# A fused metaformer block on one core: the order of three stages within a step, and the buffers and loads of the filling

## What is computed

```python
x1 = conv3x3(x[:, :12], w_pc)                      # on LayerNorm over channels
x  = conv1x1(concat([x1, x[:, 12:]]), w_in)        # 48 -> 254 channels
xf = rfft2(8x8 patches of x) * fft_w               # weights per channel and frequency
a, b = split(irfft2(xf))                           # 127 and 127 channels
x  = x_in + conv1x1(gelu(a) * b, w_out)            # 127 -> 48, residual
t  = tokens of x; q = fp8e5(LayerNorm(t))
h  = relu(f16(f16(q @ fp8e5(W1)) + b1))            # 48 -> 192
t  = t + f16(f16(fp8e5(h) @ fp8e5(W2)) + b2)       # 192 -> 48, residual
```

## Time and profile before

| | us |
|---|---|
| median of 3 runs | 762.5 |
| lowest and highest | 761.84 and 766.21 |
| the profiled execution, its own time | 763.09 |
| its span, first to last instruction | 761.3 |
| mean granted TensorE clock | 0.983 |

### The profile page before, as it was taken

One profiled execution on the slowest core, in us unless ns is written; L12 is line 12 of the kernel. 1 busy time (PEld: TensorE's weight loads), 2 busy tenths in 40 slices (PEclk: granted clock), 3 DMA queues, 4 the chain that ended last, 5 costly groups with the idle time before them and its releaser, 6 DMA issues.

```text
span 761.3 us, 20170 instructions
## 1 busy us (share of the span) xinstructions
PE 683.0 (90%) x6571; PEld 506.1 (66%) x6571; DVE 594.9 (78%) x1128; ACT 549.0 (72%) x1090; POOL 484.5 (64%) x356
## 2 busy tenths in 40 slices
PE   1349999999999999989999999999999999999952
PEld 1137776777777777667777777777777777776720
DVE  4616788888888888978888888888888888887751
ACT  3134477877878877867888777878788887766764
POOL 2544657777767777767767777776876776743342
PEclk9999999999999999999999999999999999999985
DMA  3343314443334333344344333334434342231001
GB/s 71 68 98 70 79 35 98 99 101 101 74 93 99 98 82 80 87 105 101 67 100 97 97 76 80 94 100 102 101 66 100 96 99 77 63 97 44 22 22 42
DMA packets 46501, 62.36 MB, mean 82 GB/s; under 512 B 19039, under 2 KB 34871, under 8 KB 46391
## 3 DMA queue, kind: packets, MB, share of 16 engines
q1 hardware_dynamic: 46151, 60.94, 33.1%
q10 hardware_dynamic: 240, 0.05, 0.1%
HBM read 44.62 MB, written 16.35 MB: 80 GB/s over the span
## 4 chain that ended last, share of the span: by engine, by line
PE 64%; issue 12%; ACT 8%; DVE 7%; DMA 3%; POOL 2%; SPq 2%; ACTq 1%; POOLq 0%; DVEq 0%
PE mixp L461 15%; PE inva L474 11%; PE invb L479 11%; PE misc L488 7%; PE misc L534 5%; ACT hid L687 4%; PE misc L507 3%; DVE zl L852 3%; PE misc L633 3%; PE misc L516 2%; ACT zh L731 2%; PE misc L611 2%; PE misc L560 2%; PE misc L575 1%; DVE gmix L863 1%
## 5 line engine op out<-in xcount | busy, mean ns | idle before, releaser
L863 DVE TENSOR_TENSOR gmix<-mixp,freq_w 128x508 f32<-128x508 f32 x256 | 163.6, 681 | 38.0 <-PE mixp L461 37.5
L474 PE MATMUL inva<-inv,gmix 128*127 128x128 f32 x1024 | 135.6, 275 | 1.6 <-DVE gmix L863 1.6
L678 ACT ACTIVATE hid<-misc 128x512 f16<-128x512 f32 x192 | 102.0, 621 | 47.3 <-PE misc L534 47.3
L479 PE MATMUL invb<-inv,gmix 128*127 128x128 f32 x1024 | 134.5, 274 | 0.0
L461 PE MATMUL mixp<-win,zh 60*128 60x254 f16 x1024 | 120.7, 273 | 15.3 <-DVE zl L852 13.1
L474 PEld LDWEIGHTS inva<-inv,gmix 128*127 128x127 f32 x1024 | 129.6, 192 | 5.2 <-issue 3.6
L479 PEld LDWEIGHTS invb<-inv,gmix 128*127 128x127 f32 x1024 | 123.8, 191 | 0.0
L1036 POOL TENSOR_TENSOR st<-st,neg_half 128x16 f32<-128x16 f32 x32 | 94.5, 2954 | 45.3 <-DVE st L953 45.3
L461 PE MATMUL mixp<-win,zl 60*128 60x254 f16 x1024 | 119.4, 268 | 0.0
L1067 POOL TENSOR_TENSOR st<-st,neg_half 128x16 f32<-128x16 f32 x32 | 92.8, 2900 | 37.5 <-DVE st L989 37.5
L687 ACT ACTIVATE hid<-hid 128x512 fp8e5<-128x512 f16 x192 | 106.8, 636 | 0.0
(11 more groups left out here) (104 smaller groups left out, 1146.9 us busy)
## 6 DMA issues: line engine op xcount, KB each, us to landing
xin<-in_x_dram SPq DMA_DIRECT2D x64, 192.0 KB, 3.4
xres<-in_x_dram SPq DMA_DIRECT2D x64, 192.0 KB, 4.2
out_dram<-ob SPq DMA_DIRECT2D x64, 192.0 KB, 3.5
taps<-cz_scratch SPq DMA_DIRECT2D x32, 292.5 KB
crm<-rm_scratch SPq DMA_DIRECT2D x64, 96.0 KB
cz_scratch<-cz SPq DMA_DIRECT2D x64, 48.8 KB
cx<-in_x_dram SPq DMA_DIRECT2D x32, 96.0 KB
rm_scratch<-rm_t SPq DMA_DIRECT2D x128, 4.0 KB
```

The source lines that it names most:

```text
L474: mm = pe.matmul(inva[0:HID, q * PX:(q + 1) * PX], gmix[:, s % 2, q, 0:HID], inv[:], start=True, stop=True, skip_group_check=True)
L479: mm = pe.matmul(invb[0:HID, q * PX:(q + 1) * PX], gmix[:, s % 2, q, HID:HID2], inv[:], start=True, stop=True, skip_group_check=True)
L678: act.activation(hid16[:, 3 * c + g, :], bank[banks[g]][:], ACT.Copy).then_inc(hid16_ready, 1)
L863: dve.tensor_tensor(gmix[:, s % 2, 2 * q:2 * q + 2, 0:HID2], mixp[q][:, 0:2 * HID2].rearrange("p (e c) -> p e c", e=2), freq_w[:], ALU.mul ...
```

## The change

Within a turn:

- ScalarE: the high halves `zh` are copied ahead of the conversions to `hid8`; the three conversions become one instruction of 128x1536 elements, here and at the other place.
- VectorE: both low halves `zl` (with the mean between them) come ahead of the tokens `qpix`; `weigh(t, 0)` comes ahead of `gate(t, 4, 3)` and of the bias on `y16`.
- TensorE: `mix(t, 0)` comes ahead of FFN2.

In the filling, and in the buffers: `xpix`, `cx` and `crm` get two buffers, and the waits are loosened by one turn (VectorE's three waits ahead of its first sum by six more); the loads of weights are regrouped over SyncE's and ScalarE's queues and over the turns; the padding's zeros go out in turn 1; the biases are loaded behind the row statistics of turn 1.

```diff
-        xpix = sb("xpix", [128, PAIRS, 128])
+        xpix = sb("xpix", [128, 2, PAIRS, 128])
...
-        cx = sb("cx", [CC * CG, 2 * W])
-        crm = sb("crm", [CC * CG, 2, 2 * W])
+        cx = sb("cx", [CC * CG, 2, 2 * W])
+        crm = sb("crm", [CC * CG, 2, 2, 2 * W])
...
@@ -305,7 +305,7 @@
 
             def load_cx(t, behind):
                 n = at(t, behind)
-                sp.dma_start(cx[:], x_rows[image(n), n % SPI, 0:CC]).then_inc(cx_in, 16)
+                sp.dma_start(cx[:, ring(t, behind)], x_rows[image(n), n % SPI, 0:CC]).then_inc(cx_in[ring(t, behind)], 16)
 
...
             load_x((0, 0), -1)
-            sp.dma_start(raw_fft[:], fft_w.rearrange("(g p) a b u v -> p g (a b u v)", g=2)).then_inc(const_in, 16)
+            load_cx((0, 0), -1)
+            with nc.allow_non_contiguous_dma(reason="small weights, once"):
+                for part in range(2):
...
             sp.dma_start(raw_in[:, :, 0:CC], w_in_rows[:, :, 0:CC]).then_inc(const_in, 16)
             sp.dma_start(raw_in[:, :, CC:KC], w_in_rows).then_inc(const_in, 16)
-            sp.dma_start(raw_out[:], w_out.rearrange("o c a b -> o (c a b)")).then_inc(const_in, 16)
             sp.dma_start(raw_w1[:], w1.rearrange("(g p) c -> p g c", g=2)).then_inc(const_in, 16)
             sp.dma_start(raw_w2[:], w2).then_inc(const_in, 16)
-            for dst, src in ((sel, sel_d), (fwd, fwd_d), (inv, inv_d)):
-                sp.dma_start(dst[:], src).then_inc(const_in, 16)
-
-
-            def setup():
+
+            def transforms():
+
+                for dst, src in ((sel, sel_d), (fwd, fwd_d), (inv, inv_d)):
+                    sp.dma_start(dst[:], src).then_inc(const_in, 16)
+
+            def biases():
 
                 sp.wait_ge(zeroed, 1)
-                with nc.allow_non_contiguous_dma(reason="small weights, once"):
-                    for part in range(2):
-                        for dx in range(3):
-                            sp.dma_start(raw_pc[part * 3 * CC:(part + 1) * 3 * CC, dx, :],
-                                         w_pc[:, :, :, dx].rearrange("o i dy -> (i dy) o")).then_inc(const_in, 16)
-
-            def biases():
-
                 with nc.allow_non_contiguous_dma(reason="small weights, once"):
                     sp.dma_start(raw_b[:, 0:1], b1[0:128].rearrange("(p o) -> p o", o=1)).then_inc(bias_in, 16)
...
-                sp.wait_ge(csub, upto(a))
+                sp.wait_ge(csub, upto(a - 1))
                 sp.sem_inc(sp_held, 1)
                 for kind in range(2):
                     src = rm_d[ring(t, 0), kind].rearrange("(g q) w -> g (q w)", g=CG)
-                    sp.dma_start(crm[:, kind, :], src.unsqueeze(0).to_broadcast([CC, CG, 2 * W]))\
-                      .then_inc(rm_in, 16)
+                    sp.dma_start(crm[:, ring(t, 0), kind, :], src.unsqueeze(0).to_broadcast([CC, CG, 2 * W]))\
+                      .then_inc(rm_in[ring(t, 0)], 16)
 
...
                 a, n, m, k, l = (at(t, d) for d in (0, 3, 4, 5, 6))
                 early = isinstance(t[0], int) and t[1] < 2
+                if early:
+                    rows_out(t)
+                    if a == 0:
+                        transforms()
                 if live(t, -1) and not (isinstance(t[0], int) and t[1] == 0):
                     sp.wait_ge(xord_ready, upto(a))
                     sp.sem_inc(sp_held, 1)
@@ -384,17 +386,13 @@
                     sp.sem_inc(sp_held, 1)
                     load_res(t, 3)
                 if early:
-                    if a == 0:
-                        setup()
-                    rows_out(t)
-                    if a == 0:
+                    rows_in(t)
+                    if a == 1:
                         biases()
-                if live(t, 0) and not (isinstance(a, int) and a == 0):
+                if live(t, -1) and not (isinstance(t[0], int) and t[1] == 0):
                     sp.wait_ge(cmul, upto(a))
                     sp.sem_inc(sp_held, 1)
-                    load_cx(t, 0)
-                if early:
-                    rows_in(t)
+                    load_cx(t, -1)
...
                 if live(t, 4):
                     inverse(t, 4, 3)
+                if live(t, 3):
+                    mix(t, 0)
                 if live(t, 6):
...
                         mm.then_inc(y_done, 1)
-                if live(t, 3):
-                    mix(t, 0)
                 if live(t, 4):
...
-            def activations(k, c, groups):
-
-                for g in groups:
-                    act.wait_ge(relu_ready, upto(6 * k + 3 * c + g + 1))
-                    if c == 0 and g == 0:
-                        act.wait_ge(y_done, upto(2 * k))
-                    act.sem_inc(act_held, 1)
-                    act.activation(hid8[:, 3 * c + g, :], hid16[:, 3 * c + g, :], ACT.Copy, saturate=False)\
-                       .then_inc(hid8_ready, 1)
+            def activations(k, c):
+
+                act.wait_ge(relu_ready, upto(6 * k + 3 * c + 3))
+                if c == 0:
+                    act.wait_ge(y_done, upto(2 * k))
+                act.sem_inc(act_held, 1)
+                act.activation(hid8[:, 3 * c:3 * c + 3, :], hid16[:, 3 * c:3 * c + 3, :], ACT.Copy, saturate=False)\
+                   .then_inc(hid8_ready, 3)
...
+            def pads():
+
+                act.wait_ge(row_zeroed, 1)
+                for part in range(2):
...
-            act.wait_ge(row_zeroed, 1)
...
+            act.dma_start(raw_out[:], w_out.rearrange("o c a b -> o (c a b)")).then_inc(const_in, 16)
+            act.dma_start(raw_fft[:], fft_w.rearrange("(g p) a b u v -> p g (a b u v)", g=2)).then_inc(const_in, 16)
             order_x((0, 0), 0)
...
                         if q == 0:
-                            act.wait_ge(xcen_ready, upto(a))
-                            act.wait_ge(sum1, upto(a))
+                            act.wait_ge(xcen_ready, upto(a - 1))
+                            act.wait_ge(sum1, upto(a - 1))
...
-                        act.activation(xpix[:, 4 * q:4 * q + 4, 0:SPAN], src, ACT.Copy).then_inc(xpix_ready, 1)
+                        act.activation(xpix[:, ring(t, 0), 4 * q:4 * q + 4, 0:SPAN], src, ACT.Copy).then_inc(xpix_ready, 1)
...
-                if live(t, 6):
-                    activations(l, 1, range(3))
                 if live(t, 3):
                     act.wait_ge(mix_done, upto(8 * n))
                     for q in range(2):
                         act.wait_ge(coef_done, upto(2 * n + q + 1))
                         act.activation(zh[0:KSPAN, 4 * q:4 * q + 4, :].rearrange("p i c -> p (i c)"),
                                        bank[(3, 0)[q]][0:KSPAN, :], ACT.Copy).then_inc(hi_ready, 1)
+                if live(t, 6):
+                    activations(l, 1)
                 if live(t, 4):
                     gelu(t, 4, 3)
...
                 if filling and t[1] == 1:
                     rows(t, 1)
+                    pads()
                 if filling and t[1] > 0:
...
                 if live(t, 5):
-                    activations(k, 0, range(3))
+                    activations(k, 0)
...
                 st1 = st1s[:, ring(t, 0, 8)]
                 if live(t, 0):
-                    dve.wait_ge(xcen_ready, upto(a - 1))
-                    dve.wait_ge(pow1, upto(a - 1))
-                    dve.wait_ge(zpix_ready, upto(a - 1))
+                    dve.wait_ge(xcen_ready, upto(a - 7))
+                    dve.wait_ge(pow1, upto(a - 7))
+                    dve.wait_ge(zpix_ready, upto(a - 7))
                     dve.wait_ge(xpix_ready, upto(2 * a + 2))
-                    dve.tensor_reduce(st1[:, 0, :], halves(xpix)[:, :, 0:CH], AX_X, ALU.add).then_inc(sum1, 1)
+                    dve.tensor_reduce(st1[:, 0, :], halves(xpix[:, ring(t, 0)])[:, :, 0:CH], AX_X, ALU.add).then_inc(sum1, 1)
+                if live(t, 3):
+                    low_parts(t, 0)
+                if live(t, 0):
+                    dve.wait_ge(sum1, upto(a + 1))
+                    dve.tensor_scalar(st1[:, 2, :], st1[:, 0, :], 1.0 / CH, None, ALU.mult).then_inc(mean1, 1)
+                if isinstance(a, int) and a == 1:
+                    rows(t, 1)
+                if live(t, 3):
+                    low_parts(t, 1)
                 if live(t, 5):
                     dve.wait_ge(tcen_ready, upto(k + 1))
                     dve.wait_ge(pow2, upto(k + 1))
@@ -924,21 +936,12 @@
                     dve.tensor_tensor(halves(qpix)[:, :, 0:CH], tcen[:], rstd, ALU.mult, saturate=False)\
                        .then_inc(qpix_ready, 1)
                 if live(t, 3):
-                    low_parts(t, 0)
-                if live(t, 0):
-                    dve.wait_ge(sum1, upto(a + 1))
-                    dve.tensor_scalar(st1[:, 2, :], st1[:, 0, :], 1.0 / CH, None, ALU.mult).then_inc(mean1, 1)
-                if isinstance(a, int) and a == 1:
-                    rows(t, 1)
-                if live(t, 3):
-                    low_parts(t, 1)
```

(45 more changed lines are left out.)

## The result

| | before | changed |
|---|---|---|
| median, us | 762.84 (4 runs) | 788.9 (4 runs, 786.65 to 791.69) |
| ratio, 95% interval | | 1.0346 (1.0319 to 1.0373) |
| profiled execution, us | 763.09 | 788.92 |
| its span, us | 761.3 | 787.1 |
| mean granted TensorE clock | 0.983 | 0.984 |

The change makes the kernel 3.5% slower. The forecast was 784 with a range of 768 to 794.

What follows compares the result with a forecast made beforehand. TensorE, busy 90% of the span, was taken to bound the kernel, with `hidden` waiting for VectorE's residual as second limit. 763.1 + 26.3 - 1.5 - 0.5 - 3.3 = 784.1, forecast 784 us, range 768 to 794.

Steps and rivals of the forecast that it cites:

- the hole: TensorE's mix waits for the low halves `zl` 30 times, 13.1 us in all; the reordering is aimed at this.
- the two cases I had bounded: VectorE's second `zl`: ends near 4.7 us into the turn if the mean is held, else near 4.2.
- what is late next: Later FFN2 delays `y16`, bias, output sum and `hidden`; a turn gets 0.86 to 1.26 us longer, taken as 1.05.
- The hold: VectorE's first small statistic doesn't end before GpSimd's output sum does; `hidden` comes at bias + 3.84 us.
- The first rival: Faster: the small statistic gets through beside the output sum, 0.4 us less a turn, 748 in all; chance 0.09.
- 25 x 1.05 = 26.3: Steady turns 7 to 31: each 1.05 us longer as `hidden` waits for the residual, 26.3 us in all.
- turn 6: Turn that already pays a wait of `hidden` behind the output sum; nothing counted there.
- -3.3, about half: Filling: second `xpix` ends a `xcen` wait, at most 6.1 us; regrouped loads may eat it; -3.3 taken.
- the costs that I listed and did not price: Filling: weight, padding and basis loads ahead of others, later biases; may eat all the gain or cost 1 us.
- 6.1 at most: Filling: most that ending ScalarE's 6.10 us wait for `xcen` could bring the first taps forward.
- -1.5: Turns 32 to 34: nothing is held, a hole of 0.69 us and smaller ones go, -1.5 us.
- -0.5: One conversion for three: costs nothing in steady turns; at the end, where FFN2 waits for conversions, gives some 0.5 us.

Runs made afterwards that it cites:

- e1: Changed kernel with VectorE's bias on `y16` moved behind the three small statistics: 752.96 us, ratio 0.9858 to the kernel before.
- e2: Changed kernel with GpSimd's output sum moved behind the inverse square root and the copy of `rm`: 754.77 us, ratio 0.9895 to the kernel before.
- e3: Changed kernel with GpSimd's output sum over half of the columns only, everything in its place: 764.04 us in one execution.
- e4: Kernel before with one edit, VectorE's bias on `y16` behind the first weighing instead of ahead of it: 804.02 us in one execution.
- e6: Changed kernel with the loads of `raw_out` and `raw_fft` on ScalarE's queue moved behind the first reordering of rows: 785.16 us in one execution.
- e7: Changed kernel with bias behind the small statistics, `raw_out` and `raw_fft` behind the first reordering, bias loads moved from SyncE to ScalarE: 748.85 us, ratio 0.9819.
- e5: Kernel before with only the change's second buffers, loosened waits and regrouped loads; order within a turn and single conversions as before: 761.5 us, ratio 0.998.
- e8: Kernel before with only `zh` copies ahead of the conversions and both low halves ahead of the tokens: 782.24 us, ratio 1.0262.

## Why the prediction was right, and where it was off

**Right: the hole.** The prediction had the mix at 4.40 to 4.8; it came at 4.56. The mean (L925) took 0.37 in the turn shown and delayed the second `zl` by about 0.2, between the two cases I had bounded.

**Right: what is late next.** FFN2 at 5.4 to 5.8 (5.54), the bias at 7.54 to 7.95 (7.71), `hidden` at 11.4 to 11.8 (11.53), steady turns longer by 0.86 to 1.26 (1.11 on average over turns 7 to 31). The waits of `hidden` for the residual are 27, of 1.3 us on average, where I had said about 1 us in 25 turns. The hold is shown from four sides: away by VectorE's order (e1), away by GpSimd's order (e2), shorter with a shorter sum (e3), and put into the old kernel alone (e4). The first rival, "nothing is held", named the right direction for a kernel without the hold, and too high a price: it had 0.4 us less a turn and 748 in all, and e1, whose bias stands elsewhere, has 0.23 less a turn (5.7 us over turns 7 to 31), 752.96 in the median and 754.8 in its profiled execution. The Trainium skill (SBUF — State Buffer, "Who interferes with whom") says that a VectorE instruction with two SBUF inputs contends with a GpSimd one that reads SBUF, and that a reduction doesn't. The traces agree with both: the first small statistic ends with the output sum in every kernel where they meet, and the reduction between bias and statistic kept its 0.94 or 0.95 in all ten.

**Off by 2.0: the sum over turns.** The term "25 x 1.05 = 26.3" measured 27.8, and turn 6, for which I counted nothing since it already had such a wait, cost 0.55: its bias came later too.

**Off by 2.4: the filling.** The term "-3.3, about half" measured -0.9: -1.63 up to turn 3 and +0.73 in turns 3 to 5. The wait for `xcen` went as foreseen, but two of the costs that I listed and did not price took most of it back before turn 3. `raw_out` and `raw_fft` ahead of the rows: the first reordering at 8.09 instead of 6.28, and e6 gets 1.84 of it back there and 2.39 at the taps. The biases on SyncE ahead of the first store of convolved channels, in the trace of the changed kernel (reordering, store, bias conversion, GpSimd's conversion that waits for the store, first taps):

```profile
8.09 1.06 ACT L706 ACTIVATE xord<-xin 128x1024 f32<-128x1024 f32 x1 [4.97 <-DMA xin<-in_x_dram]
...
32.14 1.70 SPq L402 DMA_DIRECT2D cz_scratch<-cz  x2
...
32.51 0.17 DVE L835 CAST b<-raw_b 128x3 fp8e5<-128x3 f32 x1 [3.44 <-DMA raw_b<-in_L_ffn_b_dram]
...
35.78 0.40 POOL L1016 CAST cz<-cz 96x256 f16<-96x256 f32 x1 [3.41 <-DMA cz_scratch<-cz]
...
44.32 1.47 PE L505 MATMUL misc<-taps,wpc 72*32 72x512 f16 x12 [2.85 <-DMA taps<-cz_scratch]
```

GpSimd waits 3.41 us for a store that SyncE issues behind five bias loads, and VectorE's weight building waits 3.44 for the same loads. In e7, with both mended, the store goes out at 27.14, the conversion of the biases at 28.01, and the taps arrive at 39.45, 6.50 before those of the kernel before, where I had said 6.1 at most.

The +0.73 of turns 3 to 5 is for the most part TensorE's clock in turn 3 (+0.79), for which the prediction has no term. In that turn TensorE is idle for 2.86 us in both kernels, and busy for 17.80 before and 18.59 in the changed one with the same matmuls. A pair of the mix, twice in the kernel before and once in the changed one:

```profile
56.69 0.27 PE L461 MATMUL mixp<-win,zl 60*128 60x254 f16 x2
...
59.24 0.42 PE L461 MATMUL mixp<-win,zl 60*128 60x254 f16 x2
```
```profile
55.12 0.42 PE L459 MATMUL mixp<-win,zl 60*128 60x254 f16 x2
```

Before, the granted clock is 1.00 from 55.50 to 58.90 and 0.50 from 59.00 to 62.30, so 0.27 is the pair at 2.4 GHz and 0.42 at 1.2. The changed kernel has 0.42 in both of its first mixes of the turn, up to 59.71, and 0.28 only from 62.68 on (its windows view prints a clock of 1.00 in this early stretch; the matmuls tell more). e5, with 0.27 in both mixes, has a turn 3 of 18.82 against 20.66 and 21.45. Over the traces of e1 (21.88, TensorE busy 19.02) and e8 (18.58, busy 15.72) the spread is 3.3 us, all of it TensorE's busy time. The fall before 59.00 comes while TensorE stands idle for 1.44 (up to 59.06); e5 has the same idle time up to 57.18 and no fall. What sets the moment at which the clock rises or falls was not tested, so how much of the filling's gain a change can keep there stays open. Of the +0.52 and -0.59 of turns 4 and 5 I have no experiment.

**Off by 0.4: the end.** -1.5 and -0.5 measured -1.6 together. The merged conversion takes 1.48, as estimated (1.5), and stays hidden in the steady turn.

So 784.1 + 1.5 + 0.5 + 2.4 + 0.4 = 788.9: sizes and the clock of one turn, not the mechanism.

## What to carry to other kernels

When an instruction is moved on one engine, look at what starts later on the engines that it feeds, and at what small SBUF work of VectorE then falls under a long GpSimd instruction. An instruction of 0.17 us that ends together with a GpSimd instruction is a sign of it, and the kernel before already showed it in its steady turns, almost without paying. The cure adds no work: put the producer of the long GpSimd instruction behind the small statistics, and the same change is worth 1.4% instead of costing 3.5%.

A single turn or a single execution can mislead by some us when the clock differs in it: compare TensorE's busy time for the same matmuls before giving a difference to the change.

In a filling, the first rows come before everything else on all queues together: two weight loads, 64 KB together, on another engine's queue delayed them by 1.8 us here.

## What was not expected

The price of the hold is larger than that of the whole reordering with it: one VectorE instruction moved behind its neighbour in the old kernel (e4) costs 40 us, 804.02 against 763.63. And in e8 a TensorE that had idled for the conversions started mostly 0.25 us behind their end by the profile, as it does at the end of the other kernels where FFN2 waits for them (0.25 in all); why it was 0.40 in the turn shown I did not test.
